# Issuing the four W_e loads from ScalarE's queue instead of SyncE's, in a fused residual kernel

## The chip, the cores and the metric

The kernel runs on one core of one Trainium2 chip. The metric is the device time of one execution in microseconds (us). A core has five engines that run their own instruction streams and meet only at semaphores: TensorE (PE, with its weight loads shown apart as PEld), VectorE (DVE), ScalarE (ACT), GpSimd (POOL) and SyncE (SP). A DMA is an instruction on the queue of the engine that issues it. The transfer itself is made by 16 DMA engines, and a semaphore tells when it has landed.

## The reference

```
u      = gelu(cond_1024 @ W_proj + b_proj)             # 128 x 512
W_u, W_e = weight_matrix[:512], weight_matrix[512:]     # 512 x 512 each
logits = (u @ W_u)[:, None, :] + einsum('bnd,dc->bnc', x, W_e)
out    = x + logits                                     # x: 128 x 128 x 512, float32
```

## The kernel before

The residual x is folded into the product: the kernel adds the identity to W_e and multiplies x by W_e + I. It computes each product in three passes, with x and the weights split into a high part (`hi`, `w_hi`, type fp32r) and a rest (`lo`, `w_lo`).

The 128 positions n of x are worked in two parts. The **head** is the first 8 positions, in 4 chunks of 2. The rest are 30 **quads** of 4 positions each, which use a Strassen-like scheme of seven half-size products (m1 to m7, all through the helper at L691 to L695), with operands s1 to s4 made by DVE and POOL and sums t of the quarters of W_e made by POOL.

Chunk 0 of the head is special. It is loaded as plain rows (`direct`, two DMAs at L240), which PE transposes with the identity (`flip`, L612) into PSUM; ACT makes its high part (L352) and DVE its rest (L544). Chunks 1 to 3 and the quads are loaded in a permuted order by four DMAs each (L231 for the head, L236 for the quads), and DVE transposes them in blocks (`turn_chunk`, `turn_quad`, L471). ACT then makes their high part (L348, L373), and DVE or POOL the rest (L567, L314, L318).

W_e comes in four pieces j, one DMA and one semaphore `w_e_loaded[j]` for each (L242). Of each piece DVE adds the identity (`add_identity`, L540), then DVE (j = 0, L555) or ACT (j = 1 to 3, L355) makes `w_hi`, and DVE makes `w_lo` (L549). POOL makes the sums t from all four (L301 to L306).

All DMAs stand in SP's stream, in this order: two of `direct`, four of W_e, the condition, W_proj, b_proj, the four of chunk 1, W_u, the eight of chunks 2 and 3, the eight of quads 0 and 1. SP waits for nothing before the first store, so up to there its order alone sets the order of the loads. ACT issues no DMA. ACT's stream begins with a wait for a small tile of zeros and a one-column Gelu into a scratch tile (L344), which brings the activation table in; its first real work is the high part of the flipped chunk 0.

PE's stream at the start is: 6 warm-up matmuls on zeros (L608), the flips of the two `direct` tiles (L612), 8 more warm matmuls (L608), the 24 products of chunk 0 (L627) with the flip of the condition among them, the projection of the condition (L652), chunk 1 (L658 to L660) with the flip of u in its middle, u times W_u (L675), chunks 2 and 3, and then the quads. DVE's stream is in order too: the W_e pieces, the copy of the flipped condition `cond_t` (L564), the transposes of chunk 1 (L471), its rest (L567), and so on. The bias (u @ W_u) is copied at L574, and only then DVE evacuates chunks 0 and 1 (L482) and transposes the first quad. ACT seeds the PSUM banks of the first quad with the bias (L404, L412).

Of the kernel before, what the change touches and what calls it, by code (L numbers as in the profile page):

```python
# [21 lines left out]
def build_cond_residual(nc, x, cond, weight_matrix, w_proj, b_proj, out):  # L22
# [18 lines left out]
    NJ = D // P  # L41
# [10 lines left out]
    w_e_dram = weight_matrix[D:2 * D, :].rearrange("(p j) c -> p j c", j=NJ)  # L52
# [4 lines left out]
    with ExitStack() as ctx:  # L57
        def sb(name, shape, dt=F32):
            return ctx.enter_context(nc.sbuf_tensor(name, shape, dt))

        def sem(name):
            return ctx.enter_context(nc.semaphore(name))
# [10 lines left out]
        w_e = sb("w_e", [P, NJ, C])  # L73
# [67 lines left out]
        w_e_loaded = [sem(f"w_e_loaded{j}") for j in range(NJ)]  # L141
# [75 lines left out]
        def raw_rows(buf, count):  # L217
            return buf[:, 0:count * TILE].rearrange("p (m n w) -> p m n w", m=NM, n=count)

        def head_chunk(c):  # L220
            return head_raw[:, c * T * TILE:(c + 1) * T * TILE].rearrange("p (m n w) -> p m n w", m=NM, n=T)
# [5 lines left out]
        @block.sync  # L227
        def _(sp):
            def load_head(c):
                for q in range(NQ):  # L230
                    sp.dma_start(head_chunk(c)[Q * q:Q * (q + 1)],  # L231
                                 x_dram[q, :, :, c * T:(c + 1) * T, :]).then_inc(head_loaded[c], 16)

            def load_quad(k, p):
                for q in range(NQ):
                    sp.dma_start(raw_rows(quad_raw[p], QUAD)[Q * q:Q * (q + 1)],  # L236
                                 x_dram[q, :, :, bass.ds(HEAD + k * QUAD, QUAD), :]).then_inc(quad_loaded[p], 16)

            for t in range(T):
                sp.dma_start(direct[:, t, :], x[:, t, :]).then_inc(direct_loaded[t], 16)  # L240
            for j in range(NJ):
                sp.dma_start(w_e[:, j, :], w_e_dram[:, j, :]).then_inc(w_e_loaded[j], 16)  # L242
            sp.dma_start(cond_sb[:, :], cond).then_inc(cond_loaded, 16)
            sp.dma_start(w_proj_sb[:, :, :], w_proj_dram).then_inc(w_proj_loaded, 16)
            sp.dma_start(b_proj_sb[:, :], b_proj_rows).then_inc(b_proj_loaded, 16)
            load_head(1)
            sp.dma_start(w_u[:, :, :], w_u_dram).then_inc(w_u_loaded, 16)
            load_head(2)
            load_head(3)
            load_quad(0, 0)  # L250
            load_quad(1, 1)

            sp.wait_ge(evacuated, 2)
            sp.dma_start(out[:, 0:QUAD, :], y[0][:, :, :]).then_inc(stored[0], 16)
            sp.wait_ge(a22_turned, 1)
            load_quad(2, 0)
            sp.wait_ge(evacuated, HEAD_CHUNKS)
            sp.dma_start(out[:, QUAD:2 * QUAD, :], y[1][:, :, :]).then_inc(stored[1], 16)

            def period(k, p, load, store):  # L260
                if load:

                    sp.wait_ge(a22_turned, k + 1)
                    load_quad(k + 2, p)
                if store:
                    sp.wait_ge(c12_out, k)
                    sp.wait_ge(c11_out, k)
                    sp.wait_ge(c21_out, k)
                    sp.dma_start(out[:, bass.ds(HEAD + (k - 1) * QUAD, QUAD), :],
                                 y[1 - p][:, :, :]).then_inc(stored[1 - p], 16)  # L270

            period(1, 1, True, True)
            with sp.Fori(1, QUADS // 2 - 1) as it:
                for p in range(2):
                    period(it * 2 + p, p, True, True)
            period(QUADS - 2, 0, False, True)
            period(QUADS - 1, 1, False, True)

            n = N - QUAD
            sp.wait_ge(c11_out, QUADS)  # L280
            sp.wait_ge(c12_out, QUADS)
            sp.dma_start(out[:, n:n + T, :], y[1][:, upper, :]).then_inc(last_stored, 16)
            sp.wait_ge(c22_out, QUADS)
            sp.dma_start(out[:, n + T:n + QUAD, right], y[1][:, lower, right]).then_inc(last_stored, 16)
            sp.wait_ge(c21_out, QUADS)
            sp.dma_start(out[:, n + T:n + QUAD, left], y[1][:, lower, left]).then_inc(last_stored, 16)
            sp.wait_ge(stored[0], 16 * (QUADS // 2 + 1))
            sp.wait_ge(stored[1], 16 * (QUADS // 2))
            sp.wait_ge(last_stored, 16 * 3)
# [50 lines left out]

        @block.scalar
        def _(act):
            act.wait_ge(zeros_ready, 1)
            act.activation(scratch[:, :], zeros[:, 0:1], ACT.Gelu).then_inc(scratch_written, 1)  # L344

# [259 lines left out]
        def _(pe):  # L605
# [71 lines left out]

            pe.wait_ge(head_lo_ready, 1)
            *_, last = plain(2)
            last.then_inc(multiplied, 1)  # L680

            pe.wait_ge(head_lo_ready, 2)
            pe.wait_ge(bias_ready, 1)
            *_, last = plain(3)
            last.then_inc(multiplied, 1)

# [94 lines left out]
```

## Time and profile before

| | us |
|---|---|
| median of 3 runs | 352.43 (352.33 to 352.7) |
| the profiled execution, device time | 352.34 |
| its span, first to last instruction | 350.4 |
| PE busy in the span | 340.2 |
| POOL busy | 280.7 |
| DVE busy | 260.8 |
| ACT busy | 239.9 |

The span lies 1.9 us under the device time of the same execution. Times of single steps are counted from the start of the span. A row of a timeline gives start, duration, engine, line and operation; "[2.12 <-X]" behind it says that the engine sat idle that long before it and what released it.

### The profile page before, as it was taken

To read this page: it belongs to the slowest core of one execution; us is meant where nothing else is said; L and a number is where in the kernel's file an instruction comes from. 1 tells how busy PE (TensorE), PEld (TensorE's weight loads), DVE (VectorE), ACT (ScalarE), POOL (GpSimd) and SP (SyncE) were. 2 spreads that over 40 slices of the span, in tenths; PEclk is the share of its full clock that TensorE was granted. 3 is DMA by queue.
4 is the path that set the end of the run, shared out by engine and by line. 5 is a ranking of instruction groups with operands and counts; after the bars stand their busy time and mean duration, and the time that the engine had idled before them with its cause. 6 is when DMAs were issued, how large, how long until landed. Compare 5 with 4: busy or idle time off the path is not lost.

```text
span 350.4 us, 7724 instructions
## 1 busy us (share of the span) xinstructions
PE 340.2 (97%) x2662; PEld 327.4 (93%) x2662; DVE 260.8 (74%) x297; ACT 239.9 (68%) x406; POOL 280.7 (80%) x196
## 2 busy tenths in 40 slices
PE   8969899999999999999999999999999999999995
PEld 4646699999999999999999999999999999999994
DVE  2575988877777788777778887777788777778811
ACT  3251577777777877777788777777877777778741
POOL 0865698898888888989888888898888988888850
PEclk9999999999999999999999999999999999999999
DMA  6999669879977888898787889988787899776214
GB/s 205 309 215 171 208 166 228 202 161 239 236 212 203 213 202 189 182 239 231 201 217 190 208 186 203 239 213 214 198 213 195 176 228 235 213 201 189 120 60 181
DMA packets 73223, 70.88 MB, mean 202 GB/s; under 512 B 2816, under 2 KB 67840, under 8 KB 68992
## 3 DMA queue, kind: packets, MB, share of 16 engines
q1 hardware_dynamic: 73216, 70.79, 80.2%
q8 instruction: 4, 0.07, 0.1%
q14 instruction: 3, 0.02, 0.0%
HBM read 37.22 MB, written 33.55 MB: 202 GB/s over the span
## 4 chain that ended last, share of the span: by engine, by line
PE 89%; DVE 4%; DMA 3%; SPq 2%; ACT 1%; issue 1%; DVEq 0%; ACTq 0%
PE banks L691 29%; PE banks L695 29%; PE banks L693 29%; DMA head_raw<-in_x 3%; DVE work L471 1%; PE banks L675 1%; DVE y L482 1%; SPq L231 1%; PE banks L658 1%; PE banks L660 1%; PE banks L659 1%; SPq L242 0%; DVE lo L567 0%; ACT hi L348 0%; DVE banks L471 0%
## 5 line engine op out<-in xcount | busy, mean ns | idle before, releaser
L691 PE MATMUL banks<-t_hi,hi 128*128 128x256 f32 x480 | 135.9, 283 | 0.9 <-DVE y L534 0.9
L693 PE MATMUL banks<-t_lo,hi 128*128 128x256 f32 x480 | 135.8, 283 | 0.0
L695 PE MATMUL banks<-t_hi,lo 128*128 128x256 f32 x480 | 135.8, 283 | 0.0
L691 PE MATMUL banks<-w_hi,hi 128*128 128x256 f32 x360 | 102.0, 283 | 1.3 <-ACT banks L404 1.3
L693 PE MATMUL banks<-w_lo,hi 128*128 128x256 f32 x360 | 101.9, 283 | 0.0
L695 PE MATMUL banks<-w_hi,lo 128*128 128x256 f32 x360 | 101.9, 283 | 0.0
L471 DVE STREAM_TRANSPOSE work<-quad_raw 128x1024 f32<-128x1024 f32 (+1 forms) x60 | 97.2, 1620 | 0.0
L691 PEld LDWEIGHTS banks<-t_hi,hi 128*128 128x128 f32 x480 | 92.1, 192 | 1.0 <-issue 1.0
L693 PEld LDWEIGHTS banks<-t_lo,hi 128*128 128x128 f32 x480 | 92.1, 192 | 0.0
L695 PEld LDWEIGHTS banks<-t_hi,lo 128*128 128x128 f32 x480 | 92.1, 192 | 0.0
L318 POOL TENSOR_TENSOR lo<-work,hi 128x1024 fp32r<-128x1024 f32 x30 | 72.5, 2418 | 24.5 <-ACT hi L373 24.4
L381 ACT CAST hi<-work 128x512 fp32r<-128x512 f32 x120 | 68.6, 619 | 16.5 <-DVE work L521 8.6
L691 PEld LDWEIGHTS banks<-w_hi,hi 128*128 128x128 f32 x360 | 69.1, 192 | 1.7 <-issue 1.7
L695 PEld LDWEIGHTS banks<-w_hi,lo 128*128 128x128 f32 x360 | 69.1, 192 | 0.0
L693 PEld LDWEIGHTS banks<-w_lo,hi 128*128 128x128 f32 x360 | 69.1, 192 | 0.0
L321 POOL TENSOR_TENSOR work<-work 128x512 f32<-128x512 f32 x30 | 38.9, 1298 | 19.4 <-DVE work L521 19.4
L529 DVE TENSOR_TENSOR y<-banks,snap_rows 128x512 f32<-128x512 f32 x30 | 20.8, 692 | 41.9 <-PE banks L695 41.9
L424 ACT COPY banks<-banks 128x512 f32<-128x512 f32 x30 | 17.1, 570 | 46.9 <-PE banks L695 46.9
L373 ACT CAST hi<-work 128x1024 fp32r<-128x1024 f32 x30 | 31.6, 1055 | 15.1 <-DVE work L471 15.1
L329 POOL TENSOR_TENSOR lo<-work,hi 128x512 fp32r<-128x512 f32 x30 | 39.2, 1308 | 0.0
L332 POOL TENSOR_TENSOR lo<-work,hi 128x512 fp32r<-128x512 f32 x30 | 39.2, 1306 | 0.0
L323 POOL TENSOR_TENSOR lo<-work,hi 128x512 fp32r<-128x512 f32 x30 | 39.0, 1299 | 0.0
(70 smaller groups left out, 426.4 us busy)
## 6 DMA issues: line engine op xcount, KB each, us to landing
out<-y SPq DMA_DIRECT2D x31, 1024.0 KB, 4.6
quad_raw<-in_x SPq DMA_DIRECT2D x120, 256.0 KB, 5.7
head_raw<-in_x SPq DMA_DIRECT2D x12, 128.0 KB, 8.7
w_e<-in_L_cond_weight_matrix SPq DMA_DIRECT2D x4, 256.0 KB, 5.7
w_proj_sb<-in_L_cond_W_proj SPq DMA_DIRECT2D x1, 1024.0 KB, 9.3
w_u<-in_L_cond_weight_matrix SPq DMA_DIRECT2D x1, 1024.0 KB, 12.2
head_raw<-in_x SPq DMA_DIRECT2D x2, 256.0 KB, 2.9
out<-y SPq DMA_DIRECT2D x1, 512.0 KB, 2.6
```

Source lines behind the costliest of these rows:

```text
L318: pool.tensor_tensor(slot(lo[p], UP, 2), a_up[p], slot(hi[p], UP, 2).bitcast(F32), ALU.subtract).then_inc(up_lo, 1)
L321: pool.tensor_tensor(s4[p], a12[p], s2[p], ALU.subtract).then_inc(s4_ready, 1)
L323: pool.tensor_tensor(slot(lo[p], S2), s2[p], slot(hi[p], S2).bitcast(F32), ALU.subtract).then_inc(s2_lo, 1)
L329: pool.tensor_tensor(slot(lo[p], S3), s3[p], slot(hi[p], S3).bitcast(F32), ALU.subtract).then_inc(s3_lo, 1)
L332: pool.tensor_tensor(slot(lo[p], A22), a22[p], slot(hi[p], A22).bitcast(F32), ALU.subtract).then_inc(a22_lo, 1)
L373: act.copy(slot(hi[p], UP, 2), a_up[p]).then_inc(up_hi, 1)
L381: act.copy(slot(hi[p], at), source).then_inc(done, 1)
L471: return dve.transpose(out_, in_)
L529: dve.tensor_tensor(y[p][:, upper, right], c_bank[p], snap2[p][:, :, :], ALU.add).then_inc(c12_out, 1)
L691: pe.matmul(psum[:, t, :], a_hi[:, 2 * j + t, :], b_hi[:, j, :], start=False, stop=False, skip_group_check=True)
L693: pe.matmul(psum[:, t, :], a_hi[:, 2 * j + t, :], b_lo[:, j, :], start=False, stop=False, skip_group_check=True)
L695: last = pe.matmul(psum[:, t, :], a_lo[:, 2 * j + t, :], b_hi[:, j, :], start=False, stop=(j == T - 1), skip_group_check=True)
```

## The change

The loop over the four pieces of W_e leaves SP's stream, where it stood between the two loads of `direct` and the load of the condition, and becomes the first thing in ACT's stream, ahead of the wait for the zeros and the small Gelu. Sizes, destinations and semaphores stay as they were; no wait is added or removed.

```diff
@@ block.sync
             for t in range(T):
                 sp.dma_start(direct[:, t, :], x[:, t, :]).then_inc(direct_loaded[t], 16)
-            for j in range(NJ):
-                sp.dma_start(w_e[:, j, :], w_e_dram[:, j, :]).then_inc(w_e_loaded[j], 16)
             sp.dma_start(cond_sb[:, :], cond).then_inc(cond_loaded, 16)
             sp.dma_start(w_proj_sb[:, :, :], w_proj_dram).then_inc(w_proj_loaded, 16)
             sp.dma_start(b_proj_sb[:, :], b_proj_rows).then_inc(b_proj_loaded, 16)
@@ block.scalar
         def _(act):
+            for j in range(NJ):
+                act.dma_start(w_e[:, j, :], w_e_dram[:, j, :]).then_inc(w_e_loaded[j], 16)
             act.wait_ge(zeros_ready, 1)
             act.activation(scratch[:, :], zeros[:, 0:1], ACT.Gelu).then_inc(scratch_written, 1)
```

## Rows read from the trace of the kernel before

**Rows 1.** The page: busy us, share of the span, instructions of each engine.
```profile
PE 340.2 (97%) x2662; PEld 327.4 (93%) x2662; DVE 260.8 (74%) x297; ACT 239.9 (68%) x406; POOL 280.7 (80%) x196
```

**Rows 2.** Waits of TensorE, whole run: total us, times, longest us.
```profile
PE banks L658 <- DVE lo L567: 2.9, 1, 2.9
PE banks L691 <- ACT banks L404: 1.3, 1, 1.3
```

**Rows 3.** Windows: length, each engine's busy us (instructions), PEclk, DMA share, GB/s.
```profile
44.00:347.00 303.00, 302.12 (x2518) 301.93 (x2516) 233.82 (x264) 223.62 (x381) 257.04 (x177) 1.00 0.79 201
```

**Rows 4.** The chain that ended last, part: start us, us, what.
```profile
7.79 9.31 DMA head_raw<-in_x
17.12 2.11 DVE work L471 x2
...
21.61 0.50 PE banks L658
```

**Rows 5.** Timeline of SP's queue from 0 to 9 us.
```profile
0.74 0.87 SPq L240 DMA_DIRECT2D head_raw<-in_x  x2
1.65 1.85 SPq L242 DMA_DIRECT2D w_e<-in_L_cond_weight_matrix  x4
...
5.36 3.07 SPq L231 DMA_DIRECT2D head_raw<-in_x  x4
8.47 1.78 SPq L247 DMA_DIRECT2D w_u<-in_L_cond_weight_matrix  x1
```

**Rows 6.** Windows, columns as in rows 3, from 2 to 12 us.
```profile
2.00:3.00 1.00, 1.00 (x4) 0.41 (x3) 0.00 (x0) 0.23 (x2) 0.00 (x0) 1.00 0.83 289
3.00:4.00 1.00, 1.00 (x5) 0.33 (x4) 0.00 (x0) 0.00 (x0) 0.00 (x0) 1.00 0.80 281
4.00:5.00 1.00, 1.00 (x6) 1.00 (x6) 0.00 (x0) 0.13 (x1) 0.00 (x0) 1.00 0.93 162
5.00:6.00 1.00, 1.00 (x6) 0.66 (x5) 0.00 (x0) 0.73 (x2) 0.00 (x0) 1.00 0.47 158
6.00:7.00 1.00, 1.00 (x6) 0.41 (x5) 0.00 (x0) 0.31 (x1) 0.00 (x0) 1.00 0.85 293
7.00:8.00 1.00, 0.76 (x4) 0.15 (x2) 0.77 (x3) 0.00 (x0) 0.00 (x0) 1.00 0.94 311
8.00:12.00 4.00, 3.51 (x13) 2.39 (x14) 4.00 (x10) 1.76 (x3) 1.78 (x1) 1.00 1.02 399
```

**Rows 7.** DMA issues of the page: KB each, median us from issue to landing.
```profile
w_e<-in_L_cond_weight_matrix SPq DMA_DIRECT2D x4, 256.0 KB, 5.7
head_raw<-in_x SPq DMA_DIRECT2D x2, 256.0 KB, 2.9
```

**Rows 8.** Timeline of the engines from 0 to 19 us, the steps that matter.
```profile
0.74 1.28 ACT L344 ACT_TABLE_LOAD   x1 [0.74 <-PEq L771]
...
4.87 0.58 ACT L352 CAST hi<-banks 128x512 fp32r<-128x512 f32 x1 [2.63 <-PE banks L612]
...
8.11 0.73 PE L627 MATMUL banks<-w_hi,hi 128*128 128x512 f32 x2 [0.35 <-DVE w_hi L555]
...
14.31 0.69 DVE L564 COPY cond_t<-banks 128x512 f32<-128x512 f32 x1 [1.78 <-PE banks L612]
...
15.06 3.70 PE L652 MATMUL banks<-w_proj_sb,cond_t 128*128 128x512 f32 x8
```

**Rows 9.** Matmuls of L608 by form, 5.4 to 6.2 us: busy us, mean ns.
```profile
L608 PE MATMUL banks<-zeros 128*128 128x512 bf16 x2 | 1.0, 596 | 0.0
```

**Rows 10.** The same from 6.8 to 7.4 us.
```profile
L608 PE MATMUL banks<-zeros 128*128 128x512 bf16 x5 | 1.2, 379 | 0.0
```

**Rows 11.** Timeline from 22 to 32 us: chunk 2 on its way to TensorE.
```profile
22.86 2.15 DVE L471 STREAM_TRANSPOSE work<-head_raw 128x512 f32<-128x512 f32 x2 [0.70 <-DMA head_raw<-in_x]
...
26.75 4.68 POOL L314 TENSOR_TENSOR lo<-work,hi 128x1024 fp32r<-128x1024 f32 x2 [0.25 <-ACT hi L348]
...
30.71 0.79 PE L658 MATMUL banks<-w_hi,hi 128*128 128x512 f32 x1
```

## The prediction

> **What bounds the kernel now.** I read the page first: TensorE is busy for 340.2 us, 97% of the span of 350.4 [rows 1], so the question is where its other 10.2 us lie. The windows answer that: from 44 to 347 us it is busy for 302.12 of 303.00 us [rows 3]. The loop over the quads has no room that a load could give back, and whatever moves the start of the loop moves the end by the same amount. The next view is the list of TensorE's waits. Only two are worth naming: 2.9 us before the first product of chunk 1 (L658), which waits for DVE's rest of chunk 1, and 1.3 us before the first product of the quads (L691), which waits for ACT's seed [rows 2]. The rest is the start and the tail, which this change does not touch.
>
> Then the chain that ended last, to see what stands behind the 2.9 us. Back from L658 at 21.61 it goes over DVE and ACT to the transposes of chunk 1 at 17.12, and these wait for a DMA: the last of the four loads of chunk 1 was issued at 7.79 and took 9.31 us, so it landed at 7.79 + 9.31 = 17.10 [rows 4]. Ahead of it the chain runs along SP's issues from 0.74 on, with the four W_e issues among them [rows 5]. After L658 TensorE works without a gap through chunk 1 and the bias, and DVE's work behind the bias leads to the seed. **So the landing of chunk 1 sets the end of the kernel**, with 21.61 - 17.10 = 4.5 us of fixed work in between.
>
> **The change part by part.** *What SP saves.* The four W_e issues begin at 1.65 and the next DMA's issue about 1.90 us later (1.85 us in all plus a gap of 0.05) [rows 5]. The condition, W_proj, b_proj and chunk 1 are each issued 1.90 us earlier; chunk 1's last issue ends at 6.5 in place of 8.43 (5.36 + 3.07).
>
> *What that is worth in landing time.* Chunk 1's last load takes 9.31 us from issue to landing, while a `direct` load of twice its size takes 2.9 at the start [rows 4, 7]. Some 6 us of it is a queue at the DMA engines. So its landing is set by when the engines have worked off everything ahead of it, and the same bytes lie ahead before and after. What can be gained is the time in which they were not full. From 8 us on their share is 1.02 at 399 GB/s: no room [rows 6]. From 2 to 8 us the six shares leave 0.17 + 0.20 + 0.07 + 0.53 + 0.15 + 0.06 = 1.18 us of idle time, averaged over the 16 engines. With two issuers W_e is queued from 0.74, beside `direct`, and what stood behind it 1.90 us sooner; I take it that this fills the hole. Counted in bytes it is about the same: 4 to 7 us moved 162 + 158 + 293 = 613 KB, which at the 285 GB/s of the two windows before takes 2.15 us, 0.85 us less. The trace of before has nothing on a second issuer, so this is bounded from both sides. Above: 1.90 us, all that SP saves. Nothing: the hole is a delay of the memory itself, which comes back wherever W_e is read. Below nothing: no byte comes ahead of chunk 1 that was not ahead of it before, so a loss needs slower engines; if two streams cost a second hole like the one from 4 to 7 us, it is the same 0.85 us the other way. I take 1.2, since the two counts from rows lie at 1.18 and 0.85 on one side and the issue shift at 1.90 on the other.
>
> *What ACT pays.* Four issues of about 0.47 us put its table load [rows 8] from 0.74 to about 2.6, its end with the small Gelu (0.2 us more) to about 4.1. ACT's next work is the high part at 4.87, ahead of which it sits idle for 2.63 us [rows 8], so 0.75 us of cover is left and the cost is 0. If the issues take longer on ACT, that cover goes first: at the 1.78 us of the dearest issue shown here, W_u's [rows 5], four would end at 7.9 and delay the high parts by some 4.5 us; that is the upper bound, and I take the rows of the same DMA. Nothing else is queued on ACT before.
>
> *What the `direct` loads pay.* They were alone at the start, issued at 0.74 and 1.2, landing after 2.9 us each [rows 7]. Now W_e's pieces run beside them. At 285 GB/s a piece of 256 KB takes 0.92 us, so two pieces in between cost the second `direct` load 1.8 us at most and 0 at least. Its flip, the 8 warm matmuls behind it and the first product (8.11 before) then come up to 1.8 us later. On the other hand W_e is there sooner: its pieces took 5.7 us from issues at 1.65 and later [rows 5, 7], and the 0.35 us for which the first product waited for `w_hi` goes [rows 8], as do waits of this kind between the next ones. I take 1 us later at the start and about nothing at the end of chunk 0's products. What does this hit? DVE copies the flipped condition at 14.31 to 15.0 and only then may transpose chunk 1 at 17.12, so 2.1 us of cover [rows 4, 8]; TensorE's projection ends at 15.06 + 3.70 = 18.76 against 21.61, 2.85 us of cover. With chunk 1 landing 1.2 us sooner there remain 0.9 and 1.65 us, so the cost is 0. What is late next, if chunk 1 gains more than 2.1 us, is that copy: the gain ends there.
>
> *Whether it reaches the end.* Everything from 17.12 on shifts together, if the loads behind keep pace. Chunk 2's transposes waited for their landing 0.70 us at 22.86; POOL's rest of it, half of 4.68 us from 26.75, ends at 29.1, and TensorE takes it at 30.71 [rows 11]. So 1.6 us of cover, over the 1.2 even if chunk 2 lands no sooner. The 1.3 us wait for the seed is at the end of DVE's chain behind the bias and moves with it.
>
> **Sum:** 352.34 - 1.2 = 351.1 for the profiled execution; the median lies 0.09 above that, so **351.2 us**.
>
> **The rivals.** *A, the forecast:* the hole fills and chunk 1 lands 0.7 to 2.1 us sooner: 350.3 to 351.7.
>
> *B, no difference:* chunk 1 lands where it did. The long way from issue to landing speaks for it: a transfer that stands in a queue for 6 us does not care that it was issued 1.9 us sooner, and the engines' share of 0.80 to 0.93 in three of the first windows [rows 6] says that there was work while they ran slow, as if the reads of W_e were slow themselves. The one window at 0.47 speaks against it. It gives 352.4, and 351.8 to 353.1 with shifts of 0.6 us either way. The Trainium skill, "DMA: Bandwidth & Descriptors", section "Issuing engines are not separate DMA queues", holds this rival's side: all issuers share the same 16 DMA engines, and issuing from several saves only the sequencer's time. By that rule alone the gain would be nothing wherever the issue is not what is late. The shares over 1 from 8 us on agree with it, the 0.47 does not.
>
> *C, slower:* the late `direct` tiles take the place of chunk 1 as what is late. The warm matmuls of L608 took 596 ns in the pair before 6.2 us and 379 ns in the five behind 6.8 [rows 9, 10]; the page grants 1.00 throughout (the 2.4 GHz level), but by durations the engine was slow up to there. If the flips come 1.8 us late, TensorE stands idle between its warm-up and them, and the 24 products of chunk 0 may begin before it is fast. At that ratio (596 / 379 = 1.57) products that now run in 7.0 us (8.11 to 15.06, flip of the condition included) would take up to 4 us more. 1.8 + 4.0 - 2.1 of DVE's cover = 3.7 us: 356 at the worst. The point from which it decides is a `cond_t` copy 2.1 us later than now (or 0.9 if chunk 1 lands 1.2 sooner, which then merely eats the gain). For a loss of 0.7 us it takes 2.8 us. Against it: 2.1 us is much, and W_e comes sooner, which takes waits out of that same stretch. I put it at 353.1 to 356.
>
> **How the numbers follow.** A 0.50, B 0.34, C 0.16. Differences under 0.2% (0.7 us) cannot be told from none. Faster 0.50, same 0.34, slower 0.16. The range takes A whole with a little below it for a gain in which `cond_t` comes sooner too, all of B and the near part of C: 350.0 to 353.3, which leaves out about 0.07 below and 0.1 above.
>
> **What would show it.** W_e's issues stand on ACT from 0.74, about 0.43 us each, and its table load behind them. The DMA share from 2 to 8 us is near 0.95 and the window with 0.47 is gone. Chunk 1's transposes start at 15.9 and L658 at 20.4; TensorE's busy share in the loop is as before, and the wait of 1.3 us at L691 stays. `cond_t` is copied before 15.9. The forecast is wrong if the hole returns at another place (then B), if L564 starts after 16.4 (then C), or if ACT's issues take over 0.8 us each.

## The result

The changed kernel takes 357.43 us (median of 5 executions), the kernel before 352.33 us in the same comparison: a ratio of 1.0125, 95% interval 1.0087 to 1.0164 (the two medians by themselves give 1.0145, inside it). It is **slower by about 5 us**, where the forecast was 1.2 us faster with a range of 350.0 to 353.3. The span of the profiled execution went from 350.4 to 355.5 us.

The page of the kernel after, engines and DMA queues. It answers rows 1:
```profile
span 355.5 us, 7724 instructions
PE 342.6 (96%) x2662; PEld 328.0 (92%) x2662; DVE 264.2 (74%) x297; ACT 239.9 (67%) x406; POOL 280.2 (79%) x196
...
q1 hardware_dynamic: 72640, 69.74, 78.3%
q10 hardware_dynamic: 576, 1.05, 1.0%
```
ACT's loads have a queue of their own, q10. In its part of the chain that ended last (start us, us, what) the kernel after differs from rows 4 at once:
```profile
2.15 13.37 DMA w_e<-in_L_cond_weight_matrix
15.55 0.39 DVE w_e L540
15.93 5.68 DVE w_lo L549 x4
21.61 0.60 DVE cond_t L564
22.21 2.05 DVE work L471 x2
...
26.64 0.50 PE banks L658
```
Before, chunk 1's transposes waited for chunk 1's own landing at 17.10. Now chunk 1 has landed at 19.05 and the transposes still wait until 22.14, because VectorE is busy with the rests of W_e, whose last piece landed only at 15.5, 13.37 us after its issue. Chunk 1's first product moved from 21.61 to 26.64, by 5.03 us, and the span grew by 5.1. The loop and the 1.3 us at L691 are as they were.

The start in the timeline of the kernel after (columns as in rows 5 and 8):
```profile
0.74 2.16 ACTq L342 DMA_DIRECT2D w_e<-in_L_cond_weight_matrix  x4
2.93 1.28 ACT L344 ACT_TABLE_LOAD   x1 [2.93 <-issue]
4.25 2.98 SPq L231 DMA_DIRECT2D head_raw<-in_x  x4
5.66 0.72 PE L612 MATMUL banks<-ident,head_raw 128*128 128x128 f32 x4 [1.73 <-DMA head_raw<-in_x]
8.79 1.13 PE L612 MATMUL banks<-ident,head_raw 128*128 128x128 f32 x4 [2.41 <-DMA head_raw<-in_x]
9.71 3.62 PE L608 MATMUL banks<-zeros 128*128 128x512 bf16 x8
```
ACT issues all four pieces by 2.9 us, and SP issues chunk 1 from 4.25 in place of 5.36. But TensorE waits for the second `direct` tile until 8.79, and the eight warm matmuls behind it take 3.62 us, where they took 2.28 before. In the second of its two waits (1.73 and 2.41 us) TensorE's granted clock falls: it is 0.50, the 1.2 GHz level, in every window from 8 to 14 us, where the kernel before has 1.00. One of these windows (columns as in rows 6):
```profile
9.00:10.00 1.00, 1.00 (x5) 0.80 (x5) 0.39 (x1) 0.05 (x1) 0.00 (x0) 0.50 1.02 422
```

The table collects, from the semaphores' records in each trace and the timelines, when things landed or began in all kernels of this study (us from the start of the span):

```
                          direct  W_e    W_proj  chunk 1  cond_t  turn     first product  span
                          tile 2  last   landed  landed   copied  chunk 1  of chunk 1
before                     4.20    9.38  13.28   17.10    14.31   17.12    21.61          350.4
after                      8.75   15.53  14.92   19.05    21.54   22.14    26.64          355.5
e1_w_proj_held             8.89   10.94  15.85   19.95    18.70   19.98    24.49          353.4
e2_half_on_act             7.35    9.71  13.59   17.78    17.51   18.12    22.62          351.5
e3_w_e_after_direct        4.14   16.54   9.26   17.31    22.56   23.16    27.64          356.5
e4_splits_early            8.84   15.46  14.87   18.85    19.30   19.90    24.43          353.2
e5_pool_held               8.91   15.53  15.30   18.98    20.14   20.75    25.27          354.1
e6_small_w_proj            8.61   11.80  14.96   19.16    18.24   19.19    23.70          352.5
e7_w_e_alone               9.68    6.35  15.18   19.87    18.75   19.89    24.41          353.3
e8_b_proj_later            4.21    9.62  13.74   16.41    15.64   16.43    20.94          349.8
e9_chunk1_before_w_proj    8.62   12.88  17.70   15.39    18.89   19.49    24.00          352.8
e10_before_chunk1_first    4.15    9.57  15.65   13.27    14.40   15.01    19.52          348.3
e11_before_pool_held       4.17    9.44  13.30   17.28    14.21   17.30    21.78          350.6
e12_w_e_first_on_sp       10.94    8.19  15.92   19.86    21.06   21.67    26.16          355.0
e13_w_e_one_load           7.64    7.06  10.78   15.55    16.91   17.52    22.02          350.9
e14_direct_contiguous      6.92   12.53  11.98   15.64    18.54   19.14    23.63          352.4
e15_before_direct_contig.  4.12    9.14  13.10   17.03    15.15   17.05    21.57          352.0
e16_before_w_e_one_load    4.44    8.78  12.68   17.02    17.31   17.92    22.43          351.3
e17_one_load_chunk1_first  4.29   10.02  15.99   13.64    18.43   19.04    23.55          352.4
e18_after_w_e_one_load     7.23    6.63  10.38   15.20    16.48   17.09    21.59          350.5
```
In 19 of the 20 rows the span is the first product of chunk 1 plus 328.8 or 328.9 us (the other, e15, has a reason of its own, below). And that product follows the start of the transposes by 4.5 us, which is when the later of two things has happened: chunk 1 has landed, or VectorE is through with `cond_t`. So the whole study is about these two.

Each row is one execution, and it need not be a typical one: e12's was the longest of its kernel's 7, 0.98 us over the median, e4's the longest of its 10, 0.82 over, e15's lies 0.86 over, e17's 0.71 and e8's 0.55 under; all others lie within 0.4 us, and e13 ran only once. The table therefore shows what waits for what; how much a kernel gains or loses is read from the ratios, which compare with the kernel before as it ran beside that kernel (medians of 352.3 to 353.0 us). These ratios are not quotients of the medians either, and can differ from them by 0.3%.

### The profile page after: what moved, and what is told of

Read it like the earlier page. It is cut to its first block, busy times and chain, and to the rows that moved or that the text cites. A ratio compares the mean times of both kernels' runs of the same rounds, so it can differ in the third digit from the quotient of the medians.

```text
span 355.5 us, 7724 instructions
## 1 busy us (share of the span) xinstructions
PE 342.6 (96%) x2662; PEld 328.0 (92%) x2662; DVE 264.2 (74%) x297; ACT 239.9 (67%) x406; POOL 280.2 (79%) x196
## 4 chain that ended last, share of the span: by engine, by line
PE 88%; DVE 6%; DMA 4%; ACT 1%; issue 0%; ACTq 0%; DVEq 0%
PE banks L691 28%; PE banks L695 28%; PE banks L693 28%; DMA w_e<-in_L_cond_weight_matrix 4%; DVE w_lo L549 2%; DVE work L471 1%; PE banks L675 1%; DVE y L482 1%; PE banks L658 1%; PE banks L659 1%; PE banks L660 1%; ACTq L342 0%; DVE lo L567 0%; ACT hi L348 0%; DVE banks L471 0%
## 5 line engine op out<-in xcount | busy, mean ns | idle before, releaser
L691 PE MATMUL banks<-t_hi,hi 128*128 128x256 f32 x480 | 135.9, 283 | 0.9 <-DVE y L534 0.9
L691 PE MATMUL banks<-w_hi,hi 128*128 128x256 f32 x360 | 102.0, 283 | 1.3 <-ACT banks L404 1.3
L691 PEld LDWEIGHTS banks<-t_hi,hi 128*128 128x128 f32 x480 | 92.1, 192 | 1.0 <-issue 1.0
L691 PEld LDWEIGHTS banks<-w_hi,hi 128*128 128x128 f32 x360 | 69.1, 192 | 1.7 <-issue 1.7
```

Of the source, the lines that this page charges most:

```text
L691: pe.matmul(psum[:, t, :], a_hi[:, 2 * j + t, :], b_hi[:, j, :], start=False, stop=False, skip_group_check=True)
```

## The experiments

Three theories stood at the start. **Q**: W_e's last pieces lost their place ahead of W_proj in the one queue. **D**: the late `direct` tiles do it. **M**: two streams are slow in themselves.

**e1, W_proj held.**
```diff
+            sp.wait_ge(w_e_loaded[NJ - 1], 16)
             sp.dma_start(w_proj_sb[:, :, :], w_proj_dram).then_inc(w_proj_loaded, 16)
```


> The changed kernel, with one wait added: SP holds the load of W_proj (and all behind it) until the last piece of W_e has landed. Beside W_e only the two direct loads and the condition are then under way. Theory Q (the last pieces of W_e are late because W_proj, which stood behind them in one queue, now runs beside them): the last piece, which lands at 15.5 us in the changed kernel and by 9.4 in the kernel before, lands by about 9.5; VectorE copies the condition before 16 us; chunk 1 now lands about where it did or 1 to 2 us later than before because of the held queue; time 352.5 to 354.5. Theory D (the late direct tiles, 8.8 us in place of 4.2, and TensorE's slow clock behind them do it): the direct tiles are as late as in the changed kernel, and so is the end, 356.5 to 357.5. Theory M (two streams are slow in themselves, whatever stands in them): the last piece of W_e at 12 us or later, 355 to 357.

355.15 us, ratio 1.0056 (1.0028 to 1.0083). With nothing but `direct` and the condition beside it, W_e's last piece lands at 10.94, 4.6 us sooner than in the changed kernel: Q for the larger part, though not the 9.5 it expected. `cond_t` came at 18.7, not before 16, and the time is over Q's 352.5 to 354.5 (it lies in M's range, without the late last piece that M asked for). The windows of this kernel (columns as in rows 6) show what the rest is:
```profile
8.00:9.00 1.00, 0.06 (x1) 0.06 (x1) 0.24 (x1) 0.00 (x0) 0.00 (x0) 1.00 0.32 119
9.00:10.00 1.00, 1.00 (x5) 0.93 (x6) 0.40 (x1) 0.00 (x0) 0.00 (x0) 1.00 0.12 47
10.00:11.00 1.00, 1.00 (x4) 0.30 (x3) 0.28 (x1) 0.90 (x2) 0.00 (x0) 1.00 0.04 16
```
A share of 0.12 and 0.04 is the work of two DMA engines and of less than one out of 16. A load's semaphore counts up in 16 steps, which I read as one for each DMA engine. For the last piece 11 of them came by 8.50, the others at 8.79, 9.49, 9.62, 9.79 and 10.94: the piece waited 2.4 us for these stragglers. In the changed kernel the same steps come by 11.33 and then up to 15.53, in the kernel before by 8.89 and 9.38. So the 6.15 us by which the last piece is late there have two parts: 2.4 us until the eleventh step, and 3.7 us of wider spread behind it.

**e2, half of the change**: pieces 0 and 1 from ACT, 2 and 3 on SP.
```diff
+            for j in range(2, NJ):
+                sp.dma_start(w_e[:, j, :], w_e_dram[:, j, :]).then_inc(w_e_loaded[j], 16)
             sp.dma_start(cond_sb[:, :], cond).then_inc(cond_loaded, 16)
...
-            for j in range(NJ):
+            for j in range(2):
                 act.dma_start(w_e[:, j, :], w_e_dram[:, j, :]).then_inc(w_e_loaded[j], 16)
```


> Half of the change: pieces 0 and 1 of W_e from ACT, pieces 2 and 3 on SP between the direct loads and the condition. Theory Q: pieces 2 and 3 stand ahead of W_proj again, all four land by about 9.5 to 10, 352 to 353.5. Theory D: the direct loads still run beside two pieces of W_e and land at 6 to 8.8 us, 354.5 to 357. Theory M: two streams for half the bytes, half the loss, about 355.

353.30 us, ratio 0.9998 (0.9978 to 1.0017). W_e lands at 9.71, as Q says, and almost nothing is lost, though the second `direct` tile is 3.15 us late. Its span is 1.1 us longer, and its chain runs from the second `direct` tile (7.35) over the warm matmuls and chunk 0's products to `cond_t`: that is D's share at this lateness.

**e3, W_e behind the direct tiles**: ACT waits for the second tile ahead of its four issues.
```diff
+            act.wait_ge(direct_loaded[1], 16)
             for j in range(NJ):
                 act.dma_start(w_e[:, j, :], w_e_dram[:, j, :]).then_inc(w_e_loaded[j], 16)
```


> The changed kernel, with one wait added: ACT issues W_e only when the second direct tile has landed. Theory Q: the direct tiles are back near 4.2 us, but all of W_e now runs beside the condition and W_proj and starts 3.5 us later; the last piece lands at 14.5 to 17 us, 356.5 to 360. Theory D: with the direct tiles on time and TensorE's clock up as before, the loss goes: 352 to 354. Theory M: as Q.

358.45 us, ratio 1.014 (1.0099 to 1.0181). The `direct` tiles are on time (4.14), and it is the slowest kernel of all. D as the whole cause falls. W_proj, now ahead, lands at 9.26, and W_e at 16.54 by the same exchange of places.

**e4, the rests early**: VectorE's order alone.
```diff
             add_identity(2)
+            for j in range(NJ - 1):
+                split_w(j)
             add_identity(3)
-            for j in range(NJ):
-                split_w(j)
+            split_w(3)
```


> The changed kernel, with VectorE's order changed: the rests w_lo of pieces 0 to 2 are made before the wait for piece 3, not behind it. The transfers are as in the changed kernel. If the step from the last piece's landing over four rests (5.8 us, each beside a GpSimd step) to the copied condition is what carries the loss to the end, three of the rests leave the path, and the next late thing is chunk 1's landing at 19.05 us or the condition's flip on TensorE: chunk 1's first product at 23.5 to 24 in place of 26.6, 354 to 355. If it is only the landing of chunk 1 that counts: no difference, 357.4.

354.33 us, ratio 1.0029 (1.0002 to 1.0056): 3.1 us back by the medians, with the transfers unchanged, so the loss is carried by what VectorE has queued behind W_e's last piece. What is next late shows in the chain of this kernel, and it is D:
```profile
1.20 7.64 DMA head_raw<-in_x
8.88 1.12 PE banks L613 x4
10.01 3.41 PE banks L609 x8
13.42 5.36 PE banks L628 x20
18.79 0.49 PE banks L613 x4
19.30 0.69 DVE cond_t L565
```
From the second `direct` tile over its flip, the eight warm matmuls, the products of chunk 0 and the flip of the condition to `cond_t` at 19.30, behind chunk 1's landing (18.85). The first product came at 24.43, a little later than expected.

**e5, GpSimd held** until the last rest is made.
```diff
             pool.wait_ge(w_diag_ready, NJ)
+            pool.wait_ge(w_lo_ready[NJ - 1], 1)
```


> The changed kernel, with one wait added: GpSimd begins the sums of the quarters of W_e only when VectorE has made its last rest w_lo. In the changed kernel the four rests take 5.8 us beside GpSimd's sums, in the kernel before 2.5 us. If the two engines take turns at something they share, the rests take about 2.8 us again, the condition is copied about 3 us sooner, and the time is 354 to 355 (chunk 1's landing at 19.05 is next). GpSimd's four sums then end near 24, ahead of their use at 25.2. If the rests are slow for another reason (the DMA traffic), they stay at 5.8 us and the time at 357.4.

355.91 us, ratio 1.0057 (1.0027 to 1.0087), where 354 to 355 was expected. The timelines, of the kernel after:
```profile
15.84 5.77 DVE L549 TENSOR_TENSOR w_lo<-w_e,w_hi 128x512 fp32r<-128x512 f32 x4
16.02 1.66 POOL L299 TENSOR_TENSOR work<-w_e 128x512 f32<-128x512 f32 x1 [14.54 <-DVE w_e L540]
...
17.63 1.73 POOL L300 TENSOR_TENSOR work<-w_e 128x512 f32<-128x512 f32 x1
```
and of this one:
```profile
15.85 2.49 DVE L550 TENSOR_TENSOR w_lo<-w_e,w_hi 128x512 fp32r<-128x512 f32 x4
...
18.49 1.28 POOL L300 TENSOR_TENSOR work<-w_e 128x512 f32<-128x512 f32 x1 [17.01 <-DVE w_lo L550]
```
The four rests take 2.49 us without GpSimd and 5.77 with it; the two engines take turns. Only 1.4 us of the 3.3 arrives, not the 3 expected: TensorE waits for the first rest until 16.59 and then has 12 products (2.9 us) ahead of the condition's flip. The Trainium skill, "SBUF — State Buffer", section "Who interferes with whom", says that a VectorE instruction with two SBUF inputs and a GpSimd instruction that reads SBUF contend for a pair of ports that they share, and that this pair is an exclusive lock; the two traces agree with it.

**e6, W_proj in small packets.**
```diff
-            sp.dma_start(w_proj_sb[:, :, :], w_proj_dram).then_inc(w_proj_loaded, 16)
+            for j in range(NJ):
+                sp.dma_start(w_proj_sb[:, j, :], w_proj_dram[:, j, :]).then_inc(w_proj_loaded, 16)
...
-            pe.wait_ge(w_proj_loaded, 16)
+            pe.wait_ge(w_proj_loaded, 16 * NJ)
```


> The changed kernel, with W_proj loaded in four DMAs whose packets are 2 KB, as W_e's are, in place of one with packets of 8 KB. The same bytes from the same queue. Theory Q, if the DMA engines take packets from the two queues in turn: one packet of W_e then costs it the wait for 2 KB and not 8 KB of W_proj, and its last piece lands at 11 to 13.5 us in place of 15.5; 354.5 to 356. If the engines share by bytes or drain a whole queue at a time, nothing changes: 357.4. Theory D: nothing changes either.

354.29 us, ratio 1.0026 (1.0002 to 1.0051). In the timeline of this kernel:
```profile
11.82 0.40 DVE L541 TENSOR_TENSOR w_e<-w_e,ident 128x128 f32<-128x128 f32 x1 [0.40 <-DMA w_e<-in_L_cond_weight_matrix]
12.13 5.76 DVE L550 TENSOR_TENSOR w_lo<-w_e,w_hi 128x512 fp32r<-128x512 f32 x4
```
The same bytes in packets of a quarter the size, and W_e's last piece lands at 11.80 in place of 15.53. W_proj's own landing hardly moves (14.96). This is what packets taken in turn do, and neither D nor M has it. The packet records of the kernel after show the turns themselves: from 7 to 10 us 148 packets of SP's queue began (104 of them of 8 KB, 920 KB in all) and 144 of ACT's (all of 2 KB, 288 KB). The counts are equal within 3%, and the bytes are more than three to one. The Trainium skill, "DMA: Bandwidth & Descriptors", section "Queues, rings and completion order", states it: each DMA engine goes round the queues that have work, a packet at a time; the run agrees. (A packet of that page can hold several of what the profile counts as packets; how many rows make one turn, these counts don't show.) The small packets bring the eleventh step of the last piece from 11.33 to 9.31; the stragglers stay, and the last step comes 2.5 us behind it. The time falls by 3 us, a little under the range expected, to where chunk 1's landing (19.16) is the last.

**e7, W_e alone**: SP waits for W_e's last piece ahead of all its loads.
```diff
+            sp.wait_ge(w_e_loaded[NJ - 1], 16)
             for t in range(T):
                 sp.dma_start(direct[:, t, :], x[:, t, :]).then_inc(direct_loaded[t], 16)
```


> The changed kernel, with SP holding every load until the last piece of W_e has landed, so that ACT's four loads run alone. It measures whether W_e's reads are slow in themselves. In the kernel before, a direct tile of the same size lands 2.9 us after its issue, four pieces at the full rate of some 285 GB/s would land by about 6 us. If W_e is as fast as x: last piece by 6.5 us. If the slow stretch from 4 to 6 us (160 GB/s) belongs to W_e's own reads: last piece at 7.5 to 9 us. Time about 358 to 361, since all else starts late.

355.42 us, ratio 1.0067 (1.004 to 1.0093), less than expected: even with 5.6 us in which SP loads nothing, this kernel beats the changed one. W_e lands by 6.35. Neither ACT's queue nor W_e's reads are slow when they are alone.

**e9, chunk 1 ahead of W_proj**, in the changed kernel.
```diff
-            sp.dma_start(w_proj_sb[:, :, :], w_proj_dram).then_inc(w_proj_loaded, 16)
-            sp.dma_start(b_proj_sb[:, :], b_proj_rows).then_inc(b_proj_loaded, 16)
             load_head(1)
+            sp.dma_start(w_proj_sb[:, :, :], w_proj_dram).then_inc(w_proj_loaded, 16)
+            sp.dma_start(b_proj_sb[:, :], b_proj_rows).then_inc(b_proj_loaded, 16)
```


> The changed kernel, with chunk 1's four loads ahead of W_proj and b_proj on SP's queue, so that what stands beside the last pieces of W_e are packets of 512 bytes and not of 8 KB. If packets are taken in turn, W_e's last piece lands by 10 to 12 us (15.5 in the changed kernel, 11.8 with W_proj in 2 KB packets), and chunk 1 lands 3 to 5 us sooner than there, by 14 to 16. The next late thing is then TensorE, which waits for the late direct tiles (8.8 us) and for W_proj before chunk 1: about 352 to 354. If bytes are shared evenly, W_e's last piece stays near 15 us and the time near 356.

354.78 us, ratio 1.0062 (1.004 to 1.0083), a little over what was expected. Chunk 1 lands at 15.39, in time; W_e's last piece at 12.88, sooner than 15.53 but later than the 10 to 12 expected, and the rests of 5.7 us behind it end the gain.

**The same question in the kernel before.** e8 moves b_proj behind chunk 1 in the one queue:
```diff
-            sp.dma_start(b_proj_sb[:, :], b_proj_rows).then_inc(b_proj_loaded, 16)
             load_head(1)
+            sp.dma_start(b_proj_sb[:, :], b_proj_rows).then_inc(b_proj_loaded, 16)
```


> The kernel before, one queue, with the load of b_proj (256 KB as it is broadcast to 128 rows) moved behind chunk 1's four loads. If the landing of chunk 1 sets the end of the kernel before, as the prediction read it, it lands 0.7 to 1.2 us sooner and the time falls by as much: 351.1 to 351.8. If something else is as late (the copy of the condition has 2.1 us of cover), less than 0.4 us of it arrives.

352.24 us, ratio 0.9965 (0.9944 to 0.9985): faster, by 0.5 us in the medians (352.76 for the kernel before beside it) and 1.2 by the ratio. Chunk 1 lands 0.69 us sooner and the span is 0.6 shorter, at the edge of what was expected.

e10 has e9's order of loads in the one queue, and e5's wait.

> The kernel before, one queue, with chunk 1's loads ahead of W_proj and b_proj, and with GpSimd's sums held until VectorE's last rest of W_e. If the landing of chunk 1 sets the end there, it lands near 13.5 to 14.5 us in place of 17.1, and what is late next is the copy of the condition (15 us) on VectorE, or W_proj, which lands near 16.5 to 17 and holds TensorE's projection (3.7 us) ahead of chunk 1's first product: that product at 19.8 to 20.8 in place of 21.6; time 0.8 to 1.8 us under the kernel before. If W_proj is later than 17.5, nothing is won.

350.31 us, ratio 0.9936 (0.9912 to 0.996): **the fastest kernel of the study**, about 2 us under the kernel before, a little more than expected. In its chain chunk 1's landing (13.27) is no longer on the path; `cond_t` is:
```profile
15.09 2.05 DVE work L472 x2
...
19.52 0.50 PE banks L659
```
The transposes begin 2.1 us sooner, which is all the cover that `cond_t` had. The order of loads without the wait was not run, so how much of the gain needs the wait is not shown.

e11 has e5's wait alone.

> The kernel before with the one wait of the earlier run added: GpSimd's sums of W_e begin only behind VectorE's last rest. There the rests end at 12.5 us and the condition is copied at 14.3, 2.1 us ahead of the transposes of chunk 1, so a rest stage of 2.5 or of 5.8 us is hidden there or nearly so: no difference within 0.2% (352.0 to 352.7). If the rest stage mattered before the change too, 0.5 us or more faster.

352.63 us, ratio 1.0011 (0.9978 to 1.0044): no difference, as expected. The trace of the kernel before has the rests at 2.51 us even without the wait, so this run alone doesn't test the cover. The trace of e8 does: its rests take 5.77 us, `cond_t` is copied at 15.64, and chunk 1's landing at 16.41 is still the last.

**e12, one queue, W_e ahead of the direct tiles**: the four W_e loads stand first in SP's stream.

> The kernel before, one queue, with W_e's four loads ahead of the direct tiles. It asks what the slow stretch from 4 to 6 us belongs to. With W_e alone from ACT its four pieces landed by 6.35 us, with no slow stretch. If that stretch comes behind the direct loads: W_e by 6.4 us, the direct tiles by 7.7, and the condition later by some 2 us more than its bytes need. If it comes behind the first loads of any kind, it stands at 4 to 6 us again and W_e lands by 7.5 to 8.5. The direct tiles being 4 us late, as in the changed kernel, but with one queue: if that lateness alone costs time, 354 to 357; by the reading that the place of W_e's last piece was what counted, 352.3 to 353.5.

355.93 us, ratio 1.0084 (1.0052 to 1.0116), above the range of the reading it was to confirm. W_e lands at 8.19, but the second `direct` tile at 10.94 and chunk 1 at 19.86, and the chain is that of e4, from the tile over the warm matmuls to `cond_t` at 21.06. So D by itself can cost as much as Q: a tile 6.7 us late makes `cond_t` 6.75 us late. (In the changed kernel the tile is only 4.55 us late.) The slow stretch that the run asked for, some 160 GB/s from 4 to 6 us, is not there (238 and 258 GB/s), and yet W_e lands at 8.19 and not by 6.4, so what the stretch belongs to stays open. And chunk 1 is 2.8 us late with the same bytes ahead of it in a single queue, so that lateness is not of the second queue as such.

**Why the stragglers lag.** e13 loads W_e from ACT in one DMA; e18 is the same kernel, timed.
```diff
-            for j in range(NJ):
-                act.dma_start(w_e[:, j, :], w_e_dram[:, j, :]).then_inc(w_e_loaded[j], 16)
+            act.dma_start(w_e[:, :, :], w_e_dram).then_inc(w_e_loaded[0], 16)
...
-                dve.wait_ge(w_e_loaded[j], 16)
+                dve.wait_ge(w_e_loaded[0], 16)
```


> The changed kernel, with W_e loaded from ACT in one DMA of 1 MB, whose packets are 8 KB, in place of four with packets of 2 KB. It turns the question round: now the direct tiles' packets of 2 KB stand beside packets of 8 KB. If packets are taken in turn, the second direct tile lands later than the 8.75 us of the changed kernel, at 9.5 to 12, though no more bytes are asked for, and W_e lands sooner than 15.5, at 9 to 12. If bytes are shared evenly, the direct tile stays at 8.75 or comes sooner.

> The changed kernel with W_e in one load from ACT, once more and timed: the single look gave 352.76 with a span of 350.9, against 355.5 for the changed kernel's. If that is its time: 352.5 to 353.2, no slower than the kernel before by more than 0.8 us. If the look was a lucky one: 354 or more.

e13: 352.76 us in one execution. e18: 352.64 us, ratio 0.9998 (0.9978 to 1.0018). Both queues as in the change, and the loss is gone. The windows of e18:
```profile
3.00:4.00 1.00, 0.94 (x3) 0.03 (x1) 0.00 (x0) 0.00 (x0) 0.00 (x0) 1.00 1.06 436
4.00:5.00 1.00, 0.00 (x0) 0.00 (x0) 0.00 (x0) 0.00 (x0) 0.00 (x0) 1.00 0.92 381
```
436 and 381 GB/s, where the changed kernel has 211 and 238. So M falls: two streams by themselves are not slow. The direct tile lands at 7.23, sooner than in the changed kernel, although it now stands beside packets of 8 KB, so e13's first expectation for it was wrong. Turns are still taken: from 3 to 5 us 83 packets of 2 KB of SP's queue began beside 79 of 8 KB of ACT's, and the eleventh of the tile's 16 steps comes later than in the changed kernel (7.10 for 6.10). But the last step follows it by 0.1 us and not by 2.65. What the one load takes away are the stragglers, so W_e's small pieces are a cause of their own. Everything lands sooner than before the change but the direct tiles, and these take the gain back over the warm matmuls.

e14 reads the direct tiles from rows that lie side by side (chunk 0 then computes on another part of x); e15 does so in the kernel before.
```diff
-                sp.dma_start(direct[:, t, :], x[:, t, :]).then_inc(direct_loaded[t], 16)
+                sp.dma_start(direct[:, t, :], x[t, :, :]).then_inc(direct_loaded[t], 16)
```


> The changed kernel, with each direct tile read from 128 rows of x that lie side by side (another part of x, so chunk 0 computes on other data) in place of rows 256 KB apart. It asks why the slowest DMA engine lags: the second direct tile lands at 8.75 us, where the bytes asked for by two queues up to it should be through by 6. If the rows' distance makes some reads slow when they are mixed with others, the direct tiles land by 6.5 us and chunk 1 at 17 to 18 in place of 19.05; time 355 to 356.5, since W_e's last piece is still late. If the lag is of two queues or of W_e's own reads: 8.5 or later, and 357.4.

> The kernel before, with the same other reading of the direct tiles. It asks what the slow stretch from 4 to 6 us (162 and 158 GB/s) belongs to. If it is the distant rows of x, the stretch is gone (over 250 GB/s), the first piece of W_e lands at 5.5 to 6 us in place of 7.1, and chunk 1 up to 1 us sooner: 351.3 to 352. If not, no difference.

e14: 354.38 us, ratio 1.0064 (1.0046 to 1.0082), under the 355 to 356.5 expected. The lag is mostly gone: `direct` at 6.92 (6.5 expected), chunk 1 at 15.64 (17 to 18 expected), even W_e's last piece at 12.53, 3 us sooner. Its eleventh step is at 11.78, no sooner than in the changed kernel (11.33), for W_proj still runs beside it in packets of 8 KB; only the spread behind that step has shrunk, from 4.2 us to 0.75. e15: 353.02 us, ratio 1.001 (0.9973 to 1.0046), no difference; the stretch from 4 to 6 us stays at 168 and 182 GB/s.

e16 has e13's one load in the kernel before, e17 in e10.

> The kernel before, one queue, with W_e loaded in one DMA of 1 MB (packets of 8 KB) in place of four pieces of 256 KB (packets of 2 KB, each piece reading 2 KB of every 8 KB). With two queues the one load let the DMA engines run at 365 to 447 GB/s from 3 to 8 us, and chunk 1 landed at 15.55 in place of 19.05. If the slow stretch from 4 to 6 us belongs to the pieces: it is gone here too, W_e lands whole by 7.0 to 7.5 us, chunk 1 by 15 to 16 in place of 17.1, and the time falls by 1.0 to 1.9 us. If it belongs to two reads being mixed: no difference, 352.4.

> The fastest kernel so far (one queue, chunk 1 ahead of W_proj and b_proj, GpSimd's sums held; 350.3) with W_e in one load. There the chain to chunk 1's first product went over chunk 0's products and the copy of the condition, and no longer over chunk 1. Chunk 0's products wait for the first piece of W_e at 7.2; whole, W_e lands at 7.0 to 7.5, the same time, but its last quarter 2 us sooner. About 350, at best 349.5; if the start on a first piece counts, 350.3 to 351.

e16: 353.56 us, ratio 1.0031 (1.0011 to 1.0052). e17: 355.01 us, ratio 1.0069 (1.0046 to 1.0092). Both forecasts were wrong. In one queue the whole W_e lands at 8.78 and 10.02, later than the first piece of four (7.10 and 7.21) and hardly sooner, or later, than the last (9.38 and 9.57); chunk 1 is within 0.4 us of where it was. TensorE starts later (its first product in e16 at 9.79 in place of 8.11), and behind a wait of 2.83 us its clock falls: 0.50 in the windows of e16 from 11 to 14 us.

## Why the prediction was wrong

**"The landing of chunk 1 sets the end"**, with 4.5 us of fixed work behind it and a loop that passes every shift on: right for the kernel before. e8, e10 and the table's constant of 328.8 us bear it out. Right too was that the copy of the condition is late next, and that the gain ends there: e10 lands chunk 1 3.8 us sooner and gains 2.1 us of span, the cover that the prediction had named. In the changed kernel it is not chunk 1's landing that sets the end but that copy.

**What ACT pays**: right. Its issues took 2.16 us for four, the table load ended at 4.2, and nothing waited for it. What SP saves was smaller than put: chunk 1's first issue came 1.1 us sooner and its last ended at 7.23, not 1.9 us sooner and at 6.5, since the issues themselves grew longer.

**"W_e is there sooner"**: this is the step that failed most. Only its first piece came sooner (5.69 for 7.10). The last came 6.15 us later, for two reasons. In SP's queue it had stood ahead of W_proj, and on a queue of its own it takes turns with W_proj's larger packets: that is 2.4 us until 11 of its 16 steps are in. And the slowest DMA engines fall behind: that is the other 3.7 us. The two parts lean on each other. Taking W_proj away gives back 4.6 us, more than its own 2.4 (10.94 in e1; with W_proj in small packets 11.80 in e6). Leaving W_proj as it was and putting the `direct` rows side by side gives back 3.0 us (12.53 in e14). I had asked what the move puts beside `direct`, and not what it takes away from the moved loads themselves. The late piece shifts the transposes from about 19.2, where e6 has them, to 22.14: 3.0 of the 5.0 us.

**The stage behind it** has no term in the prediction: VectorE's four rests of W_e, 2.51 us in the trace of the kernel before, lay in the cover of `cond_t`. Once piece 3 is late the four rests stand between it and `cond_t`, and they took 5.77 us beside GpSimd (2.49 without it, e5). e4 and e5 took 3.1 and 1.5 us of the loss back with the transfers as they were.

**"1.8 us at most" for the direct tiles**: the second came 4.55 us later. The bound was worked out from mean rates; the landing is that of the slowest of 16 engines. The tile's eleventh step came 2.2 us later (6.10 for 3.93), a little over the bound, its last one 4.55. And 1 us later at the start with nothing at the end was wrong too: the first product came at 12.77 in place of 8.11, since the eight warm matmuls ran behind the late tile at a granted clock of 0.50.

**The 1.2 us of filled idle time**: more was moved, as forecast. From 2 to 8 us the kernel after moved 180 + 211 + 238 + 330 + 340 + 387 = 1686 KB, before 1494 [rows 6]:
```profile
2.00:3.00 1.00, 1.00 (x4) 0.42 (x3) 0.00 (x0) 0.07 (x1) 0.00 (x0) 1.00 0.77 180
3.00:4.00 1.00, 0.94 (x3) 0.03 (x1) 0.00 (x0) 1.00 (x1) 0.00 (x0) 1.00 0.87 211
4.00:5.00 1.00, 0.00 (x0) 0.00 (x0) 0.00 (x0) 0.42 (x2) 0.00 (x0) 1.00 0.94 238
5.00:6.00 1.00, 0.34 (x3) 0.37 (x4) 0.21 (x1) 0.00 (x0) 0.00 (x0) 1.00 1.01 330
6.00:7.00 1.00, 0.38 (x4) 0.19 (x2) 0.62 (x2) 0.58 (x1) 0.00 (x0) 1.00 1.05 340
7.00:8.00 1.00, 0.00 (x0) 0.00 (x0) 0.69 (x1) 0.01 (x1) 0.00 (x0) 0.99 1.02 387
```
Yet chunk 1 landed 1.95 us later, since the gain went to the fast engines and a landing waits for the slow ones. The first of the 64 steps of chunk 1's four loads came at 12.12 (12.59 before), the last at 19.05 (17.10). "It is the same 0.85 us the other way" was too small a bound below nothing. Where the stragglers are gone the forecast gain is there: chunk 1 lands 1.46 us sooner than before the change in e14 and 1.90 in e18, and then `cond_t` is what is late.

**Rival C** had the sign and a part of the mechanism: late tiles, warm matmuls at the slow clock, a late `cond_t`. With W_e's last piece out of the way `cond_t` is copied at 19.3 (e4), which is 2.8 us of span in that execution, the longest of ten, and 1.3 us by the medians. The rival lacked W_e's last piece, so its price, 356 at the worst, was short as well. The two do not add up: each ends at `cond_t`, and the later counts. No run left the eight warm matmuls out, so what they cost in the changed kernel is not measured.

**Open**: why some DMA engines lag. It takes W_e's pieces of 2 KB out of every 8 and the direct rows 256 KB apart at the same time: with either one replaced (e14, e18) the lag of chunk 1 is gone, in one queue neither matters as long as the tiles come first (e15, e16), and with W_e first it is there without a second queue (e12). What in the memory or the engines does this, no run shows.

## What to carry to other kernels

A single queue is also an order of priority. Moving a load to a second queue frees what stood behind it, and takes from the moved load its place ahead of the rest; here the two queues then went packet by packet. So list for each load, moved or not, what runs beside it afterwards, with its packet size, and price the last landing and not the mean rate. In this kernel, where the DMA engines are the bound at the start, changing the order in one queue (what is needed first goes first) was worth more than a second issuer: e10, which also held GpSimd back, gained 0.6% where the second queue lost 1.3%.

## What the runs showed of the hardware

- One load of 1 MB in rows of 8 KB and four loads that each take 2 KB of every 8 KB of the same tensor differ by a factor of 1.6 to 2.1 in throughput when a second queue runs beside them (436 and 381 GB/s from 3 to 5 us in e18, against 211 and 238 in the changed kernel). In one queue the difference is small (1125 KB from 4 to 8 us in e16, 924 in the kernel before) and brings chunk 1 only from 17.10 to 17.02.
- Two queues were served packet for packet, whatever the packets' sizes (148 to 144 packets from 7 to 10 us in the changed kernel, 83 to 79 from 3 to 5 us in e18). A landing is that of the slowest DMA engine, and the spread can be most of a delay: the last 5 of 16 steps of W_e's last piece took 0.5 us before the change and 4.2 after it.
- Whether VectorE and GpSimd take turns is not settled by the order of instructions. In the kernel before, GpSimd's first sum began 0.20 us behind VectorE's first rest, the four rests went through in 2.51 us and that sum took 3.46. In e8, with the same order and a sum that began 0.18 us behind, the rests took 5.77 us. What decides it, no run shows.
- TensorE's granted clock can fall again after it was up. In the profiled execution of e15 TensorE had waited 1.99 us for chunk 1, and some of the windows behind that read (columns as in rows 6):
```profile
22.00:23.00 1.00, 1.00 (x6) 0.82 (x5) 0.50 (x2) 0.87 (x2) 1.00 (x2) 1.00 1.22 223
23.00:24.00 1.00, 1.00 (x5) 0.74 (x4) 1.00 (x2) 0.00 (x0) 1.00 (x2) 0.51 1.22 211
...
25.00:26.00 1.00, 1.00 (x5) 0.70 (x4) 0.95 (x1) 0.00 (x0) 1.00 (x2) 0.50 1.23 205
26.00:27.00 1.00, 1.00 (x7) 0.91 (x6) 1.00 (x2) 0.32 (x1) 0.42 (x1) 0.78 1.23 215
```
That is 1.2 GHz in place of 2.4 from 23 to about 26 us, and it goes with the 1.6 us by which its span is over the table's rule (352.0 against 21.57 + 328.8 = 350.4). The kernel before waited longer at the same place, 2.85 us, and its windows from 22 to 28 us all read 1.00, so the length of that wait alone does not decide it.
